# Two recurrent layers of attention and experts on one core: the turned rows and the output projection of a batch moved from the end of one step to the units 0 and 1 of the next

## The chip, the cores and the metric

The kernel runs on one core of a Trainium2 chip. The metric is the device time of one execution in microseconds, as the median of several runs. Lower is better.

## The reference, cut to what matters

Sixteen batches of 256 tokens with 128 channels pass through two layers. Each layer normalizes its input, computes an attention `s` and a mixture of experts `g`, and adds their product to the input.

```python
x = L0_attn_x                                  # (16, 256, 128)
xn = _layernorm(x)
s = _L0_attn_ref(xn, ...)                      # differential attention, 16 heads, causal
g = _silu(_L0_ffn_ref(xn, ...))                # top 2 of 8 experts
x = x + s * g
xn = _layernorm(x)
s = _L1_attn_ref(xn, ...)                      # window of 128, 16 heads of 8
g = _silu(_L1_ffn_ref(xn, ...))
x = x + s * g

# inside _L0_attn_ref, per batch and head
att = softmax(q1 @ k1.T) - lam * softmax(q2 @ k2.T)
y = att @ v
y = (y - mean(y)) / sqrt(var(y) + EPS) * (1 - LAMBDA_INIT)     # per head of 16 values
return y.reshape(B, T, 256) @ c_w
# inside _L1_attn_ref: out = softmax(windowed scores) @ v, then out @ wo.T + bo
```

## The kernel before

Each layer runs four parts one after the other: normalization, router, experts, attention. The experts leave their outputs in a list in HBM (`list_out`), from which the attention part later gathers the two rows of each token. The change touches only the attention part, `build_attention`, which is built once for each layer.

**Steps and units.** The attention part works on one batch of 256 tokens in each step. It is a software pipeline written out for every engine by itself: the function `schedule` calls the engine's `body` for the steps -3 to 16. The steps -3 to 0 are written out, the steps 1 to 12 are a loop (`Fori`) of three turns over four steps, and the steps 13 to 16 are written out again. A step has `UNITS` units, 12 in layer 0 (two attention maps `a`) and 6 in layer 1 (one map). In each unit TensorE computes two banks of scores for the row maxima of a batch ahead (`scores_for_max`, L986 and L987) and two banks of scores of the batch of this step (`scores`, the same lines). VectorE reduces the former to maxima (`search`, L1287) and ScalarE takes the exponentials of the latter (`exp`, L1188). In most units TensorE also multiplies probabilities and values (`weigh`, L1077 and L1080), which ScalarE copies out (`copy_weighed`, L1193).

**General uses.** All other products of TensorE share two PSUM banks, `G`. They are called general uses, and they take the two banks in turn, in the order of the table `ORDER`; the number beside each name is the unit at the end of which it stands. `general` lets TensorE start a use only when the use two before it has been copied out by ScalarE (`g_free`), and ScalarE copies them in the same order. The uses are: `qk0` and `qk1`, the projections to q and k of the batch three ahead (`project_qk`, L968; copied by `copy_qk`, L1169 and L1170 in layer 1); `v`, the values of the next batch (L975); `shift`, the turned negated maxima of the next batch (`turn_shift`, L1103; copied by L1216 and L1217); `turn{a}{qb}`, the weighed sums of map `a` turned so that queries lie on partitions (`turn_weighed`, L1088; copied by L1209); `rows`, the normalized rows turned back (`turn_rows`, L1096; copied by L1202 to `yT`); and `out`, the output projection (`project_out`, L1112 and in layer 1 L1115; copied by L1229 to `s_rows`).

**What follows a use.** `divide` on VectorE (L1336, in layer 1 L1345) stands in the unit that the table `DIVIDE` gives; it waits for the last turn of its map. In layer 0 GpSimd then computes the norm of each head (`head_norm`, L849 to L867), whose last instruction L867 writes `out_rows`; `turn_rows` waits for it. In layer 1 the division itself writes `out_rows`. `gate` on GpSimd (L898 and L900) multiplies `s_rows` by the experts' activated output and adds it to `x`; in layer 1 SyncE stores the result (`store`, L944). `fetch_ffn` (L877, four gathers by GpSimd's own DMA queue) and `mix_ffn` (L886, L889) bring the experts' output of a batch.

**The stack.** The copies of q and k are split on VectorE into three bf16 pieces (`split`, L1269, L1272, L1275, in the units of the table `SPLIT`). SyncE's queue then issues twelve transfers of them to the stack (`fill_stack`, L933), and ahead of these the two transfers of the split shifts (`split_shift` L1309, `fill_shift` L939), in this order in its queue. There is one buffer of pieces, so `copy_qk` of `qk0` waits until the fill of the batch before has landed (`stacked`).

In the order of GpSimd's queue a step was: mix of the last batch, head norm of the last batch (layer 0), fetch of this batch, gate of the last batch. The head norm of a batch, its turned rows and its projection were all in the same step: in layer 0 rows and projection stood in unit 11, the last, and in layer 1 in the units 4 and 5.

## Time and profile before

| | |
|---|---|
| median of 3 runs | 1562.79 us (1559.96 to 1567.36) |
| the profiled execution | 1560.15 us |
| its span, first to last instruction | 1558.4 us |
| TensorE busy | 1080.5 us, 69% |
| VectorE busy | 797.8 us, 51% |
| ScalarE busy | 756.5 us, 49% |
| GpSimd busy | 652.9 us, 42% |
| mean granted TensorE clock | 0.855 |

The shares are averages over parts with different limits. The attention part of layer 0 lies from about 335 to 896 us, that of layer 1 from about 1195 to 1558 us. PE is TensorE, DVE VectorE, ACT ScalarE, POOL GpSimd, SP SyncE, and SPq its DMA queue. In a row of the timeline the number in square brackets is the time for which the engine stood idle before the instruction, followed by what ended the wait.

### The profile page before, as it was taken

The page shows a single profiled execution, that of the slowest core. Times are in us where ns is not written, and L with a number is a line of the kernel's source. Part 1 is how long each engine was busy: PE and PEld are TensorE (multiplying, and loading weights), DVE is VectorE, ACT ScalarE, POOL GpSimd, SP SyncE. Part 2 cuts the span into 40 slices and gives each one's busy share as a digit, 9 for nine tenths or more (in the row PEclk, how much of TensorE's full clock was granted, in tenths as well). Part 3 has the DMA queues.
Part 4 walks back from the last instruction along what each step waited for, and adds up shares of the span by engine and source line. Part 5 has one row for each costly group of instructions (what it writes and reads, how often), then busy time and mean ns, then how long its engine had stood idle before and what let it go on. Part 6 is the DMA issues. An engine that isn't in the chain of part 4 may idle for free. (4 is left out here: it accounts for less than half of the span.)

```text
span 1558.4 us, 39725 instructions
## 1 busy us (share of the span) xinstructions
PE 1080.5 (69%) x12282; PEld 821.1 (53%) x12282; DVE 797.8 (51%) x1739; ACT 756.5 (49%) x1764; POOL 652.9 (42%) x868
## 2 busy tenths in 40 slices
PE   1400899858888788888888233009996678888886
PEld 1400899835655556555654122009996355555564
DVE  5411466447667666567562054115663555555561
ACT  2070456415667566676667022005553255555564
POOL 2277100010577677677767721760002013333344
PEclk9999999958899889898898555559998599999997
DMA  6061222132322232222400002312222222222220
GB/s 175 6 191 51 63 67 69 51 88 51 83 50 51 51 86 61 51 50 58 89 10 9 7 0 85 100 55 61 67 68 58 55 50 62 63 56 59 63 55 25
DMA packets 166094, 95.52 MB, mean 61 GB/s; under 512 B 18547, under 2 KB 159749, under 8 KB 165957
## 3 DMA queue, kind: packets, MB, share of 16 engines
q1 hardware_dynamic: 157764, 76.82, 19.0%
q0 software_dynamic: 8192, 16.79, 3.8%
q8 instruction: 96, 1.57, 0.4%
q14 instruction: 42, 0.34, 0.1%
HBM read 30.19 MB, written 24.64 MB: 35 GB/s over the span
## 5 line engine op out<-in xcount | busy, mean ns | idle before, releaser
L1287 DVE TENSOR_REDUCE at_maxima<-ps 128x2 f32<-128x512 f32 (+1 forms) x576 | 372.4, 685 | 224.2 <-PE ps L987 222.2
L1188 ACT ACTIVATE at_probs<-ps 128x512 f32<-128x512 f32 x576 | 322.4, 602 | 103.2 <-PE ps L987 98.3
L986 PE MATMUL ps<-tables 64*128 64x256 bf16 (+1 forms) x2304 | 232.6, 265 | 121.9 <-DVE at_maxima L1287 50.1
L615 ACT ACTIVATE ex_hid<-ps,ex_w 128x128 f32<-128x128 f32 x576 | 164.4, 368 | 251.0 <-PE ps L585 251.0
L987 PE MATMUL ps<-stack 64*128 64x128 bf16 (+3 forms) x3072 | 269.6, 262 | 0.0
L986 PEld LDWEIGHTS ps<-tables 64*128 64x128 bf16 x2304 | 96.1, 98 | 224.5 <-issue 189.8
L987 PEld LDWEIGHTS ps<-stack 64*128 64x128 bf16 (+1 forms) x3072 | 171.2, 102 | 9.1
L577 PE MATMUL ps<-ident,ex_rows 128*128 128x128 f32 x144 | 40.2, 279 | 195.2 <-DMA ex_rows<-list_in 195.1
L522 POOL DMA_INDIRECT list_in<-ex_rows,ex_slots x128 | 125.1, 977 | 100.9 <-DVE ex_slots L628 63.4
L646 DVE COPY ex_w<-ex_weights 128x1156 f32 x144 | 109.9, 763 | 106.4 <-issue 106.4
L585 PE MATMUL ps<-ex_rowsT,ex_w 128*128 128x128 f32 x1152 | 158.3, 282 | 0.1
L595 PE MATMUL ps<-ex_w,ex_hid 128*128 128x128 f32 x1152 | 153.6, 277 | 1.2 <-DVE ex_result L653 1.2
L877 POOL DMA_INDIRECT at_chosen_y<-list_out,at_slot x128 | 124.8, 975 | 55.6 <-issue 28.9
L585 PEld LDWEIGHTS ps<-ex_rowsT,ex_w 128*128 128x128 f32 x1152 | 143.1, 196 | 2.3 <-issue 0.7
L595 PEld LDWEIGHTS ps<-ex_w,ex_hid 128*128 128x128 f32 x1152 | 141.6, 194 | 1.5 <-issue 1.5
L1077 PE MATMUL ps<-at_probs,at_v 128*32 128x256 f32 x1536 | 130.9, 414 | 0.0
L577 PEld LDWEIGHTS ps<-ident,ex_rows 128*128 128x128 f32 x144 | 21.1, 146 | 197.0 <-issue 197.0
L898 POOL TENSOR_TENSOR at_s_rows<-at_s_rows,at_silu 128x256 f32<-128x256 f32 x32 | 23.5, 734 | 194.5 <-ACT at_s_rows L1229 194.1
L864 POOL TENSOR_TENSOR at_rstd<-at_stat,at_half 128x32 f32<-128x32 f32 x16 | 89.2, 5574 | 2.9 <-POOL at_stat L862 2.9
L1080 PE MATMUL ps<-at_probs,at_v 128*32 128x128 f32 x1536 | 80.7, 283 | 0.0
L626 DVE COPY ex_rows<-xn 128x128 f32 (+1 forms) x64 | 15.2, 237 | 123.8 <-DMA list_in<-ex_rows,ex_slots 123.2
L1269 DVE TENSOR_TENSOR at_whole<-at_whole,at_pieces 128x1024 f32<-128x1024 f32 (+1 forms) x32 | 31.1, 972 | 91.5 <-ACT at_pieces L1170 69.9
(166 smaller groups left out, 1555.6 us busy)
## 6 DMA issues: line engine op xcount, KB each, us to landing
stack<-at_pieces SPq DMA_DIRECT2D x192, 128.0 KB
stack<-at_pieces SPq DMA_DIRECT2D x192, 64.0 KB, 2.0
ex_rows<-list_in SPq DMA_DIRECT2D x144, 64.0 KB, 1.8
list_out<-ex_result SPq DMA_DIRECT2D x144, 64.0 KB, 1.5
list_in<-zero_tile SPq DMA_DIRECT2D x1, 4608.0 KB, 17.7
ex_weights<-in_L_w SPq DMA_DIRECT2D x4, 1024.0 KB, 7.4
ex_weights<-in_L_w SPq DMA_DIRECT2D x16, 256.0 KB, 7.1
x<-in_L_attn_x SPq DMA_DIRECT2D x4, 512.0 KB, 6.3
```

Of the source, the lines that this page charges most:

```text
L522: nc.gpsimd.indirect_dma_start(D["list_in"], bass.IndirectOffsetOnAxis(slots[q][k][:], 0), rows[q][:], None).then_inc(scattered[q], 16)
L585: last = nc.tensor.matmul(hid_ps[q % 2][:, hb * P:(hb + 1) * P], w[q][:, W1 + hb * P:W1 + (hb + 1) * P], rowsT[q % 2][:], start=True, stop ...
L595: last = nc.tensor.matmul(out_ps[q % 2][:, 0:C], hid[q % 2][:, hb, :], w[q][:, W2 + hb * C:W2 + (hb + 1) * C], start=(hb == 0), stop=(hb = ...
L615: last = nc.scalar.activation(hid[q % 2][:, hb, :], hid_ps[q % 2][:, hb * P:(hb + 1) * P], gelu, bias=w[q][:, B1 + hb:B1 + hb + 1])
L646: nc.vector.tensor_copy(w[q][:], weights[:, bass.ds(e, 1), :].rearrange("p o w -> p (o w)"))
L864: nc.gpsimd.tensor_tensor(rstd[:], stat[:], half[:], ALU.pow).then_inc(rstd_ready, 1)
L877: nc.gpsimd.indirect_dma_start(chosen_y[t][k][:], None, D["list_out"], bass.IndirectOffsetOnAxis(slot[:, i:i + 1], 0)).then_inc(gathered, 16)
L986: return nc.tensor.matmul(fine(bank, j), R.eye[tile, j, :], mask[tile], start=(j == 0), stop=True, skip_group_check=(j > 0))
L987: return nc.tensor.matmul(bank[:, j - 2, :], left(j - 2)[tile], right(j - 2)[tile], start=False, stop=True, skip_group_check=True)
L1077: nc.tensor.matmul(strip, v[p][:, 0, h, :], pr[:, part, at:at + SEQ], start=True, stop=False)
L1188: nc.scalar.activation(probs[:, (n // 3) % 2, n % 3, i * 512:(i + 1) * 512], t_bank[i], ACT.Exp, scale=SCALE).then_inc(t_free, 1)
L1287: nc.vector.tensor_reduce(by_half[:, h0:h0 + heads, a], s_bank[i].rearrange("p (m k) -> p m k", k=P * (late + 1)), AX.X, ALU.max).then_inc ...
```

## The change

In both layers `rows` and `out` of a batch move from the end of its step to the units 0 and 1 of the next step. The two turns of a map, which stood in one unit, now stand in two units that follow each other, and the divisions stand one or two units later (layer 0: map 1 from unit 3 to 4, map 0 from 9 to 11; layer 1: from 3 to 4). The gate of a batch moves one step later with them, to the head of GpSimd's step, and so does the store. The pipeline has one more step at its end. The steps that the loop covers go from 1 to 12, three turns, to 2 to 9, two turns; the rest is written out. No instruction on data is added or removed.

```diff
     if layer == 0:
-        ORDER = (("turn10", 2), ("turn11", 2), ("v", 4), ("qk0", 5), ("qk1", 6), ("shift", 8),
-                 ("turn00", 8), ("turn01", 8), ("rows", 11), ("out", 11))
-        DIVIDE = {3: 1, 9: 0}
+        ORDER = (("rows", 0), ("out", 1), ("turn10", 2), ("turn11", 3), ("v", 4), ("qk0", 5), ("qk1", 6),
+                 ("shift", 8), ("turn00", 9), ("turn01", 10))
+        DIVIDE = {4: 1, 11: 0}
...
     else:
-        ORDER = (("qk0", 0), ("qk1", 1), ("turn00", 2), ("turn01", 2), ("shift", 3), ("v", 4), ("rows", 4), ("out", 5))
-        DIVIDE = {3: 0}
+        ORDER = (("qk0", 0), ("rows", 0), ("qk1", 1), ("out", 1), ("turn00", 2), ("turn01", 3), ("shift", 3), ("v", 4))
+        DIVIDE = {4: 0}
...
-        if name in ("rows", "out", "last", f"turn{A - 1}0", f"turn{A - 1}1"):
+        if name in ("last", f"turn{A - 1}0", f"turn{A - 1}1"):
             return 0 <= step - 1 <= LAST
+        if name in ("rows", "out"):
+            return 0 <= step - 2 <= LAST
...
-    FIRST_FULL = 1
+    FIRST_FULL = 2
+    TURNS = (LAST - 2 - FIRST_FULL) // 4
...
-            with eng.Fori(0, (LAST - 3) // 4) as j:
+            with eng.Fori(0, TURNS) as j:
...
-            for step in range(LAST - 2, LAST + 2):
+            for step in range(FIRST_FULL + 4 * TURNS, LAST + 3):
...
                 if has(step, "out"):
+                    gate(step, step - 2)
+                if has(step, "last"):
                     mix_ffn(step - 1)
-                if has(step, "rows") and layer == 0:
-                    head_norm(step - 1)
+                    if layer == 0:
+                        head_norm(step - 1)
                 if has(step, "now"):
                     fetch_ffn(step)
-                if has(step, "out"):
-                    gate(step, step - 1)
...
                 if has(step, "out") and layer == 1:
-                    store(step - 1)
+                    store(step - 2)
...
-                    turn_rows(step, step - 1)
+                    turn_rows(step, step - 2)
...
-                    copy_out(step, step - 1)
+                    copy_out(step, step - 2)
...
-                    if has(step, "out") and n == SILU - 1:
+                    if has(step, "last") and n == SILU - 1:
                         tanh_ffn(step - 1)
...
-                    if has(step, "out") and n == SILU:
+                    if has(step, "last") and n == SILU:
                         twice_silu(step - 1)
```

## Rows read from the trace of the kernel before

**Rows 1.** Busy time (instructions), clock and DMA by stage: layer 0, layer 1.

```profile
398.00:895.00 497.00, 399.99 (x5628) 268.76 (x5616) 284.40 (x475) 310.27 (x622) 359.16 (x437) 0.85 0.21 49
1241.00:1558.00 317.00, 257.85 (x3184) 172.62 (x3183) 169.46 (x366) 179.71 (x428) 114.59 (x192) 0.93 0.21 53
```

**Rows 2.** Timeline of POOL in layer 0.

```profile
430.52 1.27 POOL L854 TENSOR_TENSOR at_y<-at_y 128x512 f32<-128x512 f32 x1 [2.82 <-DVE at_y L1336]
...
592.39 1.27 POOL L854 TENSOR_TENSOR at_y<-at_y 128x512 f32<-128x512 f32 x1 [0.95 <-DVE at_y L1336]
...
609.16 1.06 POOL L867 TENSOR_TENSOR at_out_rows<-at_y,at_rstd 128x512 f32<-128x512 f32 x1 [0.18 <-POOL at_rstd L864]
...
615.07 0.94 POOL L877 DMA_INDIRECT at_chosen_y<-list_out,at_slot  x1 [0.30 <-issue]
...
618.69 1.47 POOL L886 TENSOR_TENSOR at_chosen_y<-at_chosen_y,gate 128x128 f32<-128x128 f32 x4 [0.91 <-DMA at_chosen_y<-list_out,at_slot]
...
623.50 1.27 POOL L854 TENSOR_TENSOR at_y<-at_y 128x512 f32<-128x512 f32 x1 [2.28 <-DVE at_y L1336]
```

**Rows 3.** Timeline of PE in layer 0, from the rows to the turns.

```profile
610.28 1.12 PE L1096 MATMUL ps<-ident,at_out_rows 128*128 128x128 f32 x4 [0.62 <-POOL at_out_rows L867]
612.16 2.05 PE L1112 MATMUL ps<-wo,at_yT 128*128 128x128 f32 x8 [0.77 <-ACT at_yT L1202]
614.14 0.40 PE L986 MATMUL ps<-tables 64*128 64x128 bf16 x4
...
616.32 0.29 PE L986 MATMUL ps<-tables 64*128 64x128 bf16 x4
...
619.00 1.09 PE L1088 MATMUL ps<-ident,at_weighed_t 128*128 128x128 f32 x8
```

**Rows 4.** Timeline of one step of layer 1, engines in turn by time.

```profile
1383.96 0.47 ACT L1169 ACTIVATE at_whole<-ps,bqk 128x256 f32<-128x256 f32 x1 [4.55 <-DMA stack<-at_pieces]
...
1385.43 0.40 PE L986 MATMUL ps<-tables 64*128 64x256 bf16 x4 [2.92 <-ACT at_probs L1188]
...
1386.48 1.74 PE L1088 MATMUL ps<-ident,at_weighed_t 128*128 128x128 f32 x8
...
1387.63 1.28 DVE L1287 TENSOR_REDUCE at_maxima<-ps 128x2 f32<-128x512 f32 x2
...
1392.26 0.41 DVE L1309 TENSOR_TENSOR at_shift_p<-at_shift_t,at_shift_p 16x256 bf16<-16x256 f32 x1
...
1394.28 8.47 SPq L933 DMA_DIRECT2D stack<-at_pieces  x12
...
1402.69 0.70 PE L968 MATMUL ps<-xnT,wqk 128*128 x2
...
1404.37 0.47 ACT L1169 ACTIVATE at_whole<-ps,bqk 128x256 f32<-128x256 f32 x1 [4.08 <-DMA stack<-at_pieces]
```

**Rows 5.** Timeline of ACT in layer 1: the same copy in step 2 and step 12.

```profile
1281.58 0.47 ACT L1169 ACTIVATE at_whole<-ps,bqk 128x256 f32<-128x256 f32 x1 [3.39 <-DMA stack<-at_pieces]
...
1484.90 0.47 ACT L1169 ACTIVATE at_whole<-ps,bqk 128x256 f32<-128x256 f32 x1 [3.59 <-DMA stack<-at_pieces]
```

**Rows 6.** Timeline of PE and POOL at a jump back of the loop, layer 0.

```profile
648.95 0.40 PE L986 MATMUL ps<-tables 64*128 64x128 bf16 x4 [3.57 <-issue]
...
659.41 1.27 POOL L854 TENSOR_TENSOR at_y<-at_y 128x512 f32<-128x512 f32 x1 [5.83 <-DVE at_y L1336]
```

**Rows 7.** Timeline of DVE and POOL: one add beside a split, and without.

```profile
569.00 1.22 DVE L1269 TENSOR_TENSOR at_whole<-at_whole,at_pieces 128x1024 f32<-128x1024 f32 x1
...
569.13 1.39 POOL L849 TENSOR_TENSOR at_sq<-at_sq 128x128 f32<-128x128 f32 x1 [0.18 <-POOL at_sq L849]
...
793.39 0.45 POOL L849 TENSOR_TENSOR at_sq<-at_sq 128x128 f32<-128x128 f32 x1 [0.18 <-POOL at_sq L849]
```

**Rows 8.** Timeline of PE in layer 1: two pieces of the output projection.

```profile
1396.86 0.49 PE L1112 MATMUL ps<-wo,at_yT 128*128 128x128 f32 x2
...
1549.04 0.80 PE L1112 MATMUL ps<-wo,at_yT 128*128 128x128 f32 x2
```

## The prediction

> **What bounds the kernel now.** I read the busy time of the two attention stages first [rows 1]: about 497 us of layer 0 and 317 us of layer 1, and in neither is any engine full (TensorE 400 of 497 and 258 of 317, GpSimd 359 of 497). So each step is set by a loop of waits, not by an engine's sum, and the two layers have different loops.
>
> *Layer 0.* The start of a batch's head norm on GpSimd (L854) repeats every 31.1 us; from the step that starts it at 430.52 to the one at 623.50 there are six periods and 192.98 us, one of them with the jump back of the loop in it [rows 2]. The loop is: head norm, 592.39 to 610.22, 17.8 us; then TensorE, which already waits for it, turns the rows [rows 3]; then the projection, two units more, both turns of map 1, the search of unit 3, the division, and the next head norm at 623.50, 13.3 us after the last one's end. GpSimd by itself would allow less: its fetch issues end near 616.0, gate and mix end near 621.2, so it idles 2.28 us before 623.50 [rows 2]. So the cycle is 17.8 us of GpSimd plus 13.3 us of TensorE and its neighbours, and GpSimd's own floor is 2.3 us below it.
>
> *Layer 1.* The cycle is through SyncE [rows 4]. Put zero at 1383.96, where ScalarE's first copy of q (L1169) has waited 4.55 us for the stack's transfers, the twelve of the fill before. TensorE resumes at 1.47, the search of unit 2 begins at 3.67, the split of the shifts stands at 8.30, the twelve stack issues run from 10.32 for 8.47 us, and the next zero is at 20.41. TensorE is through with its work at 1403.39, one microsecond ahead of the next zero, and at this zero it waited 2.92 us in all: what stands there, ahead of the zero, is free. Over ten steps the period is 20.33 us [rows 5].
>
> **The change in layer 0.** Rows and output projection keep their place in the loop, except that unit 0 now stands ahead of the rows and unit 3 behind them: map 1's turns end at unit 3, the division follows at unit 4. So the number of units between the end of a head norm and the next is unchanged. What goes: the wait of 0.77 us between the rows and the projection [rows 3], since unit 1 stands between them, and the wait on one spot of two turns. What stays: 1.12 us rows, 2.05 us projection, three units, 1.09 us turns, the search and division. I lay it out from the end of the head norm, with the low clock behind the wait as in the row: rows to 1.2, unit 1 to 3.4 (2.2, like unit 0 in [rows 3], 614.14 to 616.32), projection to 5.4, unit 2 to 6.4, turn to 6.95, unit 3 with its weighing to 8.8, turn to 9.35, then 3.4 us to the head norm, as from 620.1 to 623.50: 12.8 instead of 13.3. Gain 0.5 us a step, 12 steps (2 to 13): **-6 us**. Bounds: nothing, if TensorE comes late to the rows, and 2.3 us a step, -28, where GpSimd's floor is reached.
>
> GpSimd's queue keeps its order around the circle (gate, mix, head norm, fetch); only the step's border moves between fetch and gate. The gate still waits for the projection's copy, now ready about 6 us after the head norm's end, when the fetch issues (5.8 us) have just gone out. The mix behind it waits for the gathers anyway. SyncE's order is the same too.
>
> The jump back costs 3.57 us of TensorE's time [rows 6] and makes that period 35.9 instead of 31.4 us (192.98 less 35.9, over five). The loop now runs twice instead of three times over four steps, so one of two jumps goes: **-4.5 us**. The other stands ahead of the wait for the head norm instead of behind it and is half hidden: **-2 us** (0 to -3.5). By the Trainium skill (Runtime: NRT & Kernel Launch, "Instruction fetch mechanics") a taken branch breaks the sequential prefetch and forces a fetch of its target; the trace agrees, and by that rule alone the sum would hold only these terms.
>
> A second effect is the place of VectorE's splits against the head norm. At 569.00 the split L1269 runs 1.22 us, and GpSimd's add beside it takes 1.39 us, where the same add takes 0.45 in a step without splits [rows 7]. The head norm starts one unit later against unit 7, so the split now meets another of its links, and the division of map 0, moved to unit 11, can meet the last link. I take zero: as many collisions as before, at other links; the ends are -1 and +0.7 us a step, that is -12 to +8. The Trainium skill (SBUF — State Buffer, "Who interferes with whom") has this as an exclusive lock: an operation with two SBUF inputs on VectorE and a reading one on GpSimd exclude each other, and the later one blocks. By it the moved division would add its 0.69 us wherever it starts first: about +8 us, the upper end.
>
> Layer 0 sums to **-12.5 us**.
>
> **The change in layer 1.** Here unit 0 and 1 stand at the zero itself, in the stretch where everything waits for the stack. The order of uses of the two general banks becomes q/k 0, rows, q/k 1, out. Q/k 1 now takes the bank of q/k 0, so TensorE can compute it only when ScalarE has copied q/k 0, after the zero; before, it was done at 1402.69, ahead of the zero [rows 4]. Behind it the projection, which needs the copy of the rows, and that stands in ScalarE's queue behind the copy of q/k 0. Queued behind both on TensorE are the scores of unit 2, and for these VectorE's search, the shift, the fill and the next zero.
>
> At what clock? TensorE's last work ahead of the wait ended at -0.98; take out the projection (four pieces at 0.42, 1.7) and q/k 1 (0.6) and it ends at -3.3. It resumes at 0.95: 4.2 us of waiting. After 2.92 us of waiting the row at 1386.48 shows eight transposes in 1.74 us where [rows 3] has 1.09: they ran at the level of 1.2 GHz. So I take the low clock for all of the burst: q/k 1 1.2 us, the projection 2.9 (0.80 for a pair against 0.49, [rows 8]), done at 5.05; half of unit 2's scores, and the search begins at 5.6 instead of 3.67. From there on the steps are as before (turn 1 at unit 3, ahead of the shifts, costs 0.55 us, but half of the earlier turns at unit 2 is gone). That is +1.9 us a step. Steps 2 to 12 have both the fill and the projection; the last delays only half: 10.5 times 1.9 is **+20 us**. Bounds: with the clock of 2.4 GHz throughout, q/k 1 and projection end at 3.35 and the search begins at 3.95, +0.3 a step, **+3**; with the low clock also over unit 2, unit 3 and their turns, +3 a step, **+31**.
>
> The jump back lies in layer 1 ahead of the zero, so most of its 3.57 us [rows 6] is hidden now; one goes, the other hides wholly: I give -1.5 for both (0 to -3.5). The store waits for a gate that is now early in the step. The last steps (no fill) hold the same work in another order: 0.
>
> **Sum.** -12.5 + 20 - 1.5 = +6. The profiled execution took 1560.15 us (span 1558.4); its sum is 1566. The median of the runs is 2.6 us above that execution, so I state 1562.8 + 6, rounded down: **1568 us**. A difference of 0.5%, 7.8 us, is about what a measurement of this kernel can tell.
>
> **The rivals.**
> *A, the clock stays up in layer 1 (chance 0.18).* For it: the granted clock is 0.93 over the stage [rows 1], so only a small part of a step ran low. Against: the wait becomes longer. Then +3 instead of +20: -11, **1552 us**. This ends faster.
> *B, layer 0 gives nothing but the jumps and loses to collisions (0.22).* For it: the units in the loop are the same in number, GpSimd's 17.8 us stay, and a division now lies at the head norm's end. 0 - 4.5 + 6 in layer 0, +18.5 in layer 1: +20, **1583**; half of that, +13, **1576**, if only the 0.5 us a step fail. It decides when the head norm grows by 0.5 us or TensorE arrives after it.
> *C, layer 0 falls to GpSimd's floor (0.1).* For it: 2.28 us of idle ahead of 623.50. Against: only 0.77 us of waiting is seen to go. -28 - 6.5 + 18.5 = -16, **1547**.
> *D, the change moves waits only (0.05)*: both loops keep their periods, only the jumps: -7, **1556**.
> My forecast, both mechanisms as laid out, has 0.45: its own range is 1559 to 1576.
>
> **Chances.** Faster by over 0.5% (under 1555): most of A, C and a little: 0.22. Slower by over 0.5% (over 1570.6): B and the upper third of my forecast: 0.38. Same: 0.40. The range that leaves two in ten out is 1551 to 1583.
>
> **What would show it.** Layer 0: head norms 30.6 us apart within the loop, 31.4 before; no wait of the projection for the copy of the rows; TensorE still waiting for L867 at the rows. One idle stretch of 3 us on TensorE for a jump in each layer, not two. Layer 1: zeros (L1169 behind the stack's DMA) 22.2 us apart instead of 20.3; q/k 1 after the zero; L1112 in pairs of 0.8 us; the search of unit 2 at 5.6. I am wrong if the pairs take 0.49 us there, if L1169 no longer waits for the DMA, or if the head norm's 17.8 us change.

## The result, and the profile after

The changed kernel takes 1576.12 us (median of 10 runs, 1567.34 to 1578.83), the kernel before, on the same chips, 1561.3. The ratio is 1.0082, 95% interval 1.0059 to 1.0104: slower by 0.8%. The profiled execution of after has a span of 1574.0 us, 15.6 more than before.

Where the 15.6 us lie is read from four marks: the last add to `x` in layer 0, the first zero of layer 1 (step -3), the zero of step 12, the end.

| stretch | before | after | difference |
|---|---|---|---|
| start to the last add to x in layer 0 | 894.89 | 874.41 | -20.5 |
| to the first zero of layer 1 | 303.03 | 302.99 | 0 |
| the zeros of steps -3 to 12 | 286.98 | 312.75 | +25.8 |
| zero of step 12 to the end | 73.5 | 83.9 | +10.4 |

One profile of each kernel stands in this table, and layer 0 differs between kernels whose layer 0 is the same: its last add stands at 890.9 and 891.5 us in e2 and e10, which have layer 0 as in before, and at 874.7 to 877.0 in e1, e3, e4, e7 and e11, which have it as in after. So some 17 us of the 20.5 are the change, the rest is chance.

(Lines of after are 3 higher than those of before in this part: L854 is now L857, L1169 is L1172.) The windows of the two attention stages, after; columns as in [rows 1]:

```profile
399.00:877.00 478.00, 382.26 (x5611) 253.03 (x5605) 293.88 (x474) 308.20 (x620) 372.48 (x437) 0.92 0.21 51
1221.00:1574.00 353.00, 280.16 (x3182) 188.76 (x3182) 181.94 (x365) 181.44 (x428) 120.41 (x192) 0.85 0.19 48
```

The granted clock has changed places: 0.85 to 0.92 in layer 0, 0.93 to 0.85 in layer 1.

**Layer 0.** POOL of after, one head norm and what follows, against [rows 2]:

```profile
591.21 1.48 POOL L852 TENSOR_TENSOR at_sq<-at_sq 128x256 f32<-128x256 f32 x1 [0.18 <-POOL at_sq L861]
...
595.40 6.50 POOL L867 TENSOR_TENSOR at_rstd<-at_stat,at_half 128x32 f32<-128x32 f32 x1 [0.18 <-POOL at_stat L865]
602.08 1.06 POOL L870 TENSOR_TENSOR at_out_rows<-at_y,at_rstd 128x512 f32<-128x512 f32 x1 [0.18 <-POOL at_rstd L867]
...
610.80 1.47 POOL L889 TENSOR_TENSOR at_chosen_y<-at_chosen_y,gate 128x128 f32<-128x128 f32 x4
...
614.07 1.27 POOL L857 TENSOR_TENSOR at_y<-at_y 128x512 f32<-128x512 f32 x1 [0.73 <-DVE at_y L1339]
```

The head norm that began at 584.38 ends at 603.14, and the next begins at 614.07. Before, that gap was 13.3 us; now it is 10.9, and GpSimd waits only 0.73 us in it: here it is at its floor. Two waits have shrunk, the one ahead of the head norm (2.28 to 0.73 us) and the mix's wait for the gathers (0.91 us at 618.69 in [rows 2], none at 610.80). The head norm itself grew from 17.8 to 18.76. VectorE beside its power operation L867:

```profile
595.36 1.20 DVE L1278 TENSOR_TENSOR at_pieces<-at_whole,at_pieces 128x1024 bf16<-128x1024 f32 x1
```

TensorE in the same stretch, against [rows 3]:

```profile
603.20 0.65 PE L1099 MATMUL ps<-ident,at_out_rows 128*128 128x128 f32 x4 [2.12 <-POOL at_out_rows L870]
...
605.34 1.16 PE L1115 MATMUL ps<-wo,at_yT 128*128 128x128 f32 x8
...
607.42 0.66 PE L1091 MATMUL ps<-ident,at_weighed_t 128*128 128x128 f32 x4
```

Rows in 0.65 us (1.12 before), projection in 1.16 (2.05 before), both at 2.4 GHz (the granted clock is 1.00 from 603 to 607) although TensorE waited 2.12 us just ahead; no wait for the copy of the rows is left. Not every step is like this one. Of the nine periods in steps 2 to 11 that hold no jump, six are 29.7 to 30.0 us, and three are 31.6 to 32.5, with GpSimd idle for 2.1 to 2.9 us ahead of the head norm. In these three TensorE did its rows, its projection or both at 1.2 GHz, as here:

```profile
694.31 1.12 PE L1099 MATMUL ps<-ident,at_out_rows 128*128 128x128 f32 x4 [2.12 <-POOL at_out_rows L870]
...
698.19 2.08 PE L1115 MATMUL ps<-wo,at_yT 128*128 128x128 f32 x8
...
707.92 1.27 POOL L857 TENSOR_TENSOR at_y<-at_y 128x512 f32<-128x512 f32 x1 [2.86 <-DVE at_y L1339]
```

The mean of the nine is 30.5 us, against 31.4 before. The jump back, PE and POOL:

```profile
540.73 0.40 PE L989 MATMUL ps<-tables 64*128 64x128 bf16 x4 [4.31 <-issue]
...
554.42 1.27 POOL L857 TENSOR_TENSOR at_y<-at_y 128x512 f32<-128x512 f32 x1 [2.21 <-DVE at_y L1339]
```

The period with it is 33.8 us, 3.3 over that mean and 4.0 over the short ones (4.5 over the mean in before): one jump is gone, and most of the other is still paid.

**Layer 1.** The zeros of steps 2 and 12, against [rows 5]:

```profile
1262.51 0.47 ACT L1172 ACTIVATE at_whole<-ps,bqk 128x256 f32<-128x256 f32 x1 [4.94 <-DMA stack<-at_pieces]
...
1490.15 0.47 ACT L1172 ACTIVATE at_whole<-ps,bqk 128x256 f32<-128x256 f32 x1 [3.86 <-DMA stack<-at_pieces]
```

227.64 us for ten steps: 22.76 each against 20.33. But there are two kinds of step. The windows of two that follow each other, from zero to zero:

```profile
1401.10:1422.58 21.48, 16.44 (x224) 11.11 (x216) 13.30 (x26) 11.52 (x28) 8.27 (x13) 1.00 0.22 57
1422.58:1446.08 23.50, 19.61 (x208) 13.54 (x208) 12.82 (x25) 11.92 (x29) 8.28 (x13) 0.78 0.21 52
```

Where the granted clock stays at 1.00 the step takes 21.5 us, where it is 0.78 on the mean 23.5. (One step fits neither: step 6, behind the jump back, took 23.3 us at 0.97. TensorE was still catching up there, and its projection began 3.2 us after the zero instead of 1.5.) PE and DVE in the second, against [rows 4]:

```profile
1423.56 0.67 PE L971 MATMUL ps<-xnT,wqk 128*128 x2 [2.73 <-ACT at_pieces L1173]
1424.07 0.39 PE L1115 MATMUL ps<-wo,at_yT 128*128 128x128 f32 x2
...
1425.12 0.80 PE L1115 MATMUL ps<-wo,at_yT 128*128 128x128 f32 x2
...
1426.57 0.61 PE L989 MATMUL ps<-tables 64*128 64x256 bf16 x4
...
1427.63 0.69 DVE L1290 TENSOR_REDUCE at_maxima<-ps 128x2 f32<-128x512 f32 x1 [1.03 <-PE ps L990]
...
1428.39 1.11 PE L1091 MATMUL ps<-ident,at_weighed_t 128*128 128x128 f32 x4
...
1432.01 0.66 PE L1091 MATMUL ps<-ident,at_weighed_t 128*128 128x128 f32 x4
...
1433.60 0.41 DVE L1312 TENSOR_TENSOR at_shift_p<-at_shift_t,at_shift_p 16x256 bf16<-16x256 f32 x1 [0.68 <-ACT at_shift_p L1220]
```

After the wait of 2.73 us q/k 1 and the first pair run at 2.4 GHz (0.39), then everything at 1.2 GHz until about 1431.6: the rest of the burst, unit 2, its turn (1.11), unit 3. The search begins 5.05 us after the zero, the split of the shifts 11.02 (8.3 before). In a step with the clock up it stands at 9.35.

The two kinds differ in whether TensorE waits at the zero. In the six low steps (2, 3, 5, 7, 9 and 10) it waited 2.3 to 3.2 us for ScalarE's copy of q/k 0, and the clock fell 1.4 to 2.2 us after the zero. In the steps 4, 6, 8 and 11 it came late to the zero, waited less than 0.6 us, and ran at 2.4 GHz up to the shifts (in step 6 from 1.6 us after the zero on). It came late because the clock had been at 1.2 GHz in the last units of the step before, and in step 6 because of the jump back too. So a low stretch at the end of one step spares the next one its own, unless it is short, as at the end of step 9. The same steps of e7 and e11 (below) fall apart in the same way: where TensorE waited 0.8 us or more for the copy of q/k 0, the split of the shifts stands at 12.6 to 14.3 us in e7 and 10.6 to 12.9 in e11, and where it waited less than 0.6, at 11.0 to 11.7 and 9.0 to 9.2. This is read from thirty steps and was not forced by an experiment.

**The last steps.** ScalarE's row of exponentials for the keys outside (`zero_exp`, L1227) of the last batches:

```profile
1504.00 0.22 ACT L1227 ACTIVATE at_zero_exp<-at_shift 128x16 f32<-128x16 f32 x1 [2.85 <-DVE at_out_rows L1348]
...
1521.75 0.22 ACT L1227 ACTIVATE at_zero_exp<-at_shift 128x16 f32<-128x16 f32 x1 [2.94 <-DVE at_out_rows L1348]
```

It waits for the division of the batch before, which is now one unit later; before, the same waits were 2.07 and 1.66 us. TensorE is also slower here: from the zero of step 12 to the last add it is busy for 64.98 us at a granted clock of 0.86 (714 instructions), before for 58.20 us at 0.91 (704).

### The profile page after: what moved, and what is told of

It is laid out like the page before. It is cut to its first block and busy times, and to the rows that moved or that the text cites. A ratio compares the mean times of both kernels' runs of the same rounds, so it can differ in the third digit from the quotient of the medians.

```text
span 1574.0 us, 38698 instructions
## 1 busy us (share of the span) xinstructions
PE 1088.1 (69%) x12282; PEld 822.6 (52%) x12282; DVE 820.2 (52%) x1739; ACT 757.4 (48%) x1764; POOL 671.6 (43%) x868
## 3 DMA queue, kind: packets, MB, share of 16 engines
q1 hardware_dynamic: 157764, 76.82, 18.5%
## 5 line engine op out<-in xcount | busy, mean ns | idle before, releaser
L989 PE MATMUL ps<-tables 64*128 64x256 bf16 (+1 forms) x2304 | 236.3, 268 | 117.0 <-DVE at_maxima L1290 49.7
L990 PE MATMUL ps<-stack 62*128 62x256 bf16 (+3 forms) x3072 | 269.5, 262 | 0.0
L990 PEld LDWEIGHTS ps<-stack 62*128 62x128 bf16 (+1 forms) x3072 | 172.9, 103 | 12.0
L577 PEld LDWEIGHTS ps<-ident,ex_rows 128*128 128x128 f32 x144 | 21.1, 146 | 197.0 <-issue 197.0
L901 POOL TENSOR_TENSOR at_s_rows<-at_s_rows,at_silu 128x256 f32<-128x256 f32 x32 | 23.5, 734 | 229.4 <-ACT at_s_rows L1232 229.1
L867 POOL TENSOR_TENSOR at_rstd<-at_stat,at_half 128x32 f32<-128x32 f32 x16 | 96.3, 6020 | 2.9 <-POOL at_stat L865 2.9
L971 PE MATMUL ps<-xnT,wqk 128*128 128x256 f32 (+1 forms) x192 | 65.8, 462 | 29.2 <-ACT at_pieces L1173 19.8
## 6 DMA issues: line engine op xcount, KB each, us to landing
list_in<-zero_tile SPq DMA_DIRECT2D x1, 4608.0 KB, 17.7
```

Source lines behind the costliest of these rows:

```text
L867: nc.gpsimd.tensor_tensor(rstd[:], stat[:], half[:], ALU.pow).then_inc(rstd_ready, 1)
L989: return nc.tensor.matmul(fine(bank, j), R.eye[tile, j, :], mask[tile], start=(j == 0), stop=True, skip_group_check=(j > 0))
L990: return nc.tensor.matmul(bank[:, j - 2, :], left(j - 2)[tile], right(j - 2)[tile], start=False, stop=True, skip_group_check=True)
```

## The experiments

All ratios are to the kernel before on the same chip (1560.2 to 1561.8 us). "Late zero" is short for a step whose next zero comes 2.2 us or more after the last stack issue of SyncE ended; 1.6 is usual. Twelve steps (0 to 11) are counted in each kernel.

**e1, the change in layer 0 alone; e2, in layer 1 alone.** A variable `LAG` per layer takes the place of the fixed 2, with the tables of before in the other layer:

```diff
+    LAG = 2 if layer == 0 else 1        # e2: layer == 1
...
-            return 0 <= step - 2 <= LAST
+            return 0 <= step - LAG <= LAST
...
-    FIRST_FULL = 2
+    FIRST_FULL = LAG
```

> The change in layer 0 alone; layer 1 as before. Theory (two changes of opposite sign): the profile after the change has layer 0's part about 20 us shorter, so this kernel takes about 1541 us, ratio 0.987 to the kernel before. Rival (the two layers act on each other through the loop or the code's length, or the layer 0 gain is a quirk of one execution): between 1550 and 1561 us.

> The change in layer 1 alone; layer 0 as before. Theory: about +36 us, 1597 us, ratio 1.023: some 26 us up to step 12 (2.4 us a step) and 10 us in the steps 13 to 17. Rival (my recorded sum): +18.5 us, 1580 us.

Measured: e1 1550.58 us, ratio 0.9932 (0.9912 to 0.9952); e2 1591.08, ratio 1.0203 (1.0176 to 1.023). Layer 0 is a gain, layer 1 the loss, and the two add up to within 3 us (18 us against 15). e1 missed its forecast of 1541 and lies at the edge of its rival's range, that of a code that acts on the other layer by its length. Layer 0 of e1 again ends 19.5 us early (875.35). But e1 is only 11 us faster: layer 1, whose instructions are those of before, took 298.3 us between the zeros of steps -3 and 12 instead of 287.0. Its splits of the shifts stand at 8.1 us in most steps, as before; what differs is nine late zeros against one, which hold 9.8 of the 11.3 us. The DMA view of e1, from 1 us ahead of the end of the last stack issue (1367.06) to the next zero, has this in its part on queues and issues:

```profile
q1 hardware_dynamic: 747, 0.34, 34.3%
q8 instruction: 1, 0.02, 2.5%
...
stack<-at_pieces SPq DMA_DIRECT2D x2, 64.0 KB, 2.9
```

The same stretch in a step of before (1401.76 to 1404.37), whose zero came in time:

```profile
q1 hardware_dynamic: 671, 0.31, 45.3%
...
stack<-at_pieces SPq DMA_DIRECT2D x2, 64.0 KB, 2.0
```

One packet of instructions (16 KB, 0.9 to 1.6 us on one of the 16 DMA engines) is there where the stack's last transfers take 2.9 us to land, and absent where they take 2.0. Of the 20 late zeros of before, e1, e5 and e6, 16 have such a packet that starts between 0.4 us ahead of the issue's end and 0.6 us behind it; of the 28 in time none has, and the one packet in this stretch starts 1.1 us after the issue's end. The other four late zeros (steps 4 and 8 of e1 and e5) are of another kind. They stand at the jumps back, the last transfer has landed after 1.45 us as usual, and ScalarE waits for TensorE's q/k 0, which the jump holds up:

```profile
1328.10 0.47 ACT L1175 ACTIVATE at_whole<-ps,bqk 128x256 f32<-128x256 f32 x1 [2.47 <-PE ps L974]
```

In before the zeros at the two jumps are in time (1.62 and 1.75 us).

**e3, zero_exp in four buffers, waiting for the division of two batches back; e4, both turns in unit 2 and the division in unit 3 again.**

```diff
# e3
-            zero_exp = [sb(f"zero_exp{p}", [P, HEADS]) for p in range(2)]
+            zero_exp = [sb(f"zero_exp{p}", [P, HEADS]) for p in range(4)]
...
-                    lone_wait(act, divided, b - 1)
+                    lone_wait(act, divided, b - 2)
# e4
-        ORDER = (("qk0", 0), ("rows", 0), ("qk1", 1), ("out", 1), ("turn00", 2), ("turn01", 3), ("shift", 3), ("v", 4))
-        DIVIDE = {4: 0}
+        ORDER = (("qk0", 0), ("rows", 0), ("qk1", 1), ("out", 1), ("turn00", 2), ("turn01", 2), ("shift", 3), ("v", 4))
+        DIVIDE = {3: 0}
```

> The whole change, but zero_exp in layer 1 has four buffers, so that ScalarE's copy of the shifts at unit 3 waits for the division of the batch before last and no longer for the one that the change moved to unit 4. Theory (the steps after the last fill lose their 10 us because ScalarE stands behind this division for 2.9 us in each of five steps): 7 to 10 us of the 15 come back, 1566 to 1569 us. Rival (the last steps lose by the longer fall of the clock or by the order of the projection): less than 3 us come back.

> The whole change, but in layer 1 both turns stand in unit 2 and the division in unit 3 again; rows and projection stay in the units 0 and 1. Theory (the moved division makes the last steps' loss, the burst behind the stack's wait makes the rest): the last steps get back 7 to 10 us, the steps 2 to 12 lose up to 0.5 us each by four more transposes at the low clock: 1566 to 1574 us. Rival (the loss hangs on rows and projection alone): 1576 us or more.

Measured: e3 1582.08 (ratio 1.0134, 1.0108 to 1.016), e4 1580.51 (1.0105, 1.0067 to 1.0144). In e3 the stretch from step 12's zero to the last add is 74.3 us against 77.6 in after and 67.3 in before: the wait stood on the path, but it is only a third of that loss. Up to step 12 e3 took 322.6 us instead of 312.75, with the split of the shifts at about 12 us in six of the ten steps from 2 to 11. In all ten TensorE waited at the zero (2.1 to 4.3 us), so that none had the clock up throughout. e4 gains nothing in the end (79.4) and takes 318.3 ahead of it; it puts four more transposes in unit 2 besides, so it does not show the division by itself. Both missed their forecasts (1566 to 1569 and 1566 to 1574): the late division explains 3.3 us at the end and not the loss.

**e7, the products of layer 1's projection done twice.**

```diff
-                for qb in range(QB):
+                for qb in (0, 1, 0, 1) if layer else (0, 1):
```

> The kernel after, with the products of layer 1's output projection done twice (the second set writes the same bank again with the same values), so four more pairs of 0.4 to 0.8 us in each step, all in unit 1, behind the zero. My theory: whatever stands between the zero and the scores of unit 2 is on the cycle of layer 1, so the added products cost their whole time: at the pair's 0.80 us of the lower clock 1.6 us a step, and where the added work lets the clock rise earlier, a part comes back; the period of the steps 2 to 12 goes from 22.8 to 23.9 to 24.4 us, and the total from 1576 to 1588 to 1598 us. Rival: the cycle is not on TensorE there (it is on ScalarE's copies, or on the landing of the transfers), and the added work is hidden: 1576 to 1580 us. Second rival: the low clock, not the work, is what costs; with more work ahead of unit 2 the clock is back at 2.4 GHz before it, the search of unit 2 comes no later, and the time falls to 1566 to 1574 us.

Measured: 1606.52, ratio 1.0292 (1.026 to 1.0324). ACT and PE of e7 (zeros of steps 2 and 12, one burst):

```profile
1262.33 0.47 ACT L1172 ACTIVATE at_whole<-ps,bqk 128x256 f32<-128x256 f32 x1 [3.62 <-DMA stack<-at_pieces]
1507.82 0.47 ACT L1172 ACTIVATE at_whole<-ps,bqk 128x256 f32<-128x256 f32 x1 [4.30 <-DMA stack<-at_pieces]
```

```profile
1385.75 0.46 PE L1115 MATMUL ps<-wo,at_yT 128*128 128x128 f32 x2
...
1387.42 0.80 PE L1115 MATMUL ps<-wo,at_yT 128*128 128x128 f32 x2
...
1390.32 0.61 PE L989 MATMUL ps<-tables 64*128 64x256 bf16 x4
```

The period is 24.55 us, 1.8 more than after and just over the 23.9 to 24.4 forecast: the burst stands on the cycle. Here the added set stands from 1387.42 to 1390.32, 2.9 us. It did not lift the clock: unit 2 is still at 0.61. The total went above the range, because the last steps pay too (90.7 against 77.6 us), which I had not counted.

**e11, q/k 1 ahead of the rows again, so that it doesn't need q/k 0's bank.**

```diff
-        ORDER = (("qk0", 0), ("rows", 0), ("qk1", 1), ("out", 1), ("turn00", 2), ("turn01", 3), ("shift", 3), ("v", 4))
+        ORDER = (("qk0", 0), ("qk1", 1), ("rows", 1), ("out", 2), ("turn00", 2), ("turn01", 3), ("shift", 3), ("v", 4))
```

> The kernel after, with layer 1's order of uses q/k 0, q/k 1, rows, out (rows at unit 1, out at unit 2, both turns at units 2 and 3 behind it). So q/k 1 takes the other bank and can be computed ahead of the zero again, as in before; the projection, four pieces of work behind the copy of the rows, moves one unit on. My forecast's theory, that of the 2.4 us a step that layer 1 lost the burst q/k 1 plus projection at 1.2 GHz ahead of unit 2's scores is the cause: with q/k 1 out of it 0.7 to 1.2 us a step come back, and the projection still costs its 1.0 to 1.6 us ahead of the shifts: period 21.5 to 22.1 us against 22.8, total 1563 to 1570. Rival: the low clock of the first units is the cause, whatever stands in them, since TensorE waits 3 us at the zero in either order; then 22.5 to 23 us and 1573 to 1578. Second rival: the rows' wait for their bank moves behind ScalarE's copy of q/k 1 and is later than before: 1580.

Measured: 1576.77, ratio 1.0104 (1.0061 to 1.0147), the period of steps 2 to 12 22.74 us: nothing gained. The forecast (1563 to 1570) failed, and the rival of the low clock, 22.5 to 23 us and 1573 to 1578, is what came. PE of e11 in a step whose split of the shifts stands at 9.2 us, then in the next, where it stands at 12.85:

```profile
1354.85 0.46 PE L1115 MATMUL ps<-wo,at_yT 128*128 128x128 f32 x2
...
1358.85 0.66 PE L1091 MATMUL ps<-ident,at_weighed_t 128*128 128x128 f32 x4
```

```profile
1372.96 0.41 PE L1099 MATMUL ps<-ident,at_out_rows 128*128 128x128 f32 x2 [1.65 <-ACT at_pieces L1173]
...
1375.42 0.77 PE L1115 MATMUL ps<-wo,at_yT 128*128 128x128 f32 x2 [0.78 <-ACT at_yT L1205]
...
1382.59 1.12 PE L1091 MATMUL ps<-ident,at_weighed_t 128*128 128x128 f32 x4
```

The same instructions, 3.6 us apart at the split of the shifts. Counted from the zero the projection starts at 3.64 us in the first and at 3.44 in the second, so the difference arises behind it, where the clock differs: 0.46 and 0.66 against 0.77 and 1.12. Ahead of it the second step waited twice (1.65 and 0.78 us), the first, behind the jump back, did not. So not which use stands in the burst, but how much of TensorE's work between the zero and the shifts falls into the low stretch sets the step.

**e5, the change in layer 0 alone and its three splits two units later; e6, that with layer 1's zero_exp in four buffers and a loop of two turns in layer 1; e12, e6 with layer 0's loop written out.**

```diff
# e5, layer 0
-        SPLIT = {7: (0,), 8: (1,), 9: (2,)}
+        SPLIT = {9: (0,), 10: (1,), 11: (2,)}
# e6, layer 1 with the order of before
-    FIRST_FULL = LAG
+    FIRST_FULL = 2
...
-            zero_exp = [sb(f"zero_exp{p}", [P, HEADS]) for p in range(2)]
+            zero_exp = [sb(f"zero_exp{p}", [P, HEADS]) for p in range(4)]
...
-                    lone_wait(act, divided, b - 1)
+                    lone_wait(act, divided, b - 2)
# e12: no Fori in layer 0
```

> The change in layer 0 alone, as in e1_layer0_only, and there the three splits of q and k (L1269, L1272, L1275 of before) two units later, in units 9, 10 and 11 instead of 7, 8 and 9. My theory: layer 0 now runs at GpSimd's floor (period 29.8 us, GpSimd's idle time ahead of the head norm 0.7 us), and of the head norm's 18.8 us one microsecond is paid to the splits that meet its first adds and the start of its power operation. With the splits elsewhere the head norm takes 17.8 to 18.2 us, the period is 29.0 us, and over 12 steps 7 to 10 us go: 1541 to 1545 us, against 1550.6 in e1. Rival: the later fill of the stack, now starting at unit 11 instead of unit 9, holds up the scores of the next batch or the copy of its q and k, and the period stays at 29.8 or grows to 31: 1550 to 1565 us. Second rival: the splits only meet other links of the head norm, whose time stays at 18.8: 1550 us.

> As e5_layer0_split, and in layer 1, whose order of uses is that of before, zero_exp has four buffers and its copy waits for the division of two batches back instead of one; the loop of both layers starts at step 2, so it has two turns instead of three. My theory: in the last four steps of layer 1 ScalarE's wait for the division (1.7 to 2.1 us a step in before, 2.9 to 3.0 in the kernel after) stands on the path, and without it those steps are 1 us shorter each; one jump less gives 0 to 2. So 3 to 6 us under e5. Rival: the wait stands where ScalarE has time to spare, since the steps up to 12 are bound by the stack and the last by TensorE, and only the jump shows: 0 to 2 us under e5. Second rival: as in e3_four_zero, the earlier exponentials shift TensorE's clock or the fill, and layer 1 up to step 12 is 5 us longer: e5 plus 1 to 3.

> e6_layer0_split_zero with layer 0's loop written out; layer 1's loop stays. My theory: the one jump back that is left in layer 0 (the period with it is 31.9 us against 30.4) goes: 1.5 to 4 us under e6. But the program ahead of layer 1 is now longer, so the blocks of code fall elsewhere against layer 1's steps; where they fall on the end of the stack's issues, up to 8 us come back. So 1534 to 1536 us, or up to 1544, and the count of zeros that come 2.3 us or more behind the last issue must tell which (2 of 12 in e6). Rival: written-out code costs as much as the jump: 1537 to 1539 at the same count.

Measured: e5 1547.2 (0.9901, 0.987 to 0.9933), e6 1537.62 (0.9846, 0.9816 to 0.9876), e12 1534.92 (0.9846, 0.9806 to 0.9887). e6 and e12 beat both kernels.

In e5 the head norm fell further than expected (16.4 to 17.8 us, here 17.55), but layer 0 ended where it did in e1 (874.58 against 875.35). POOL and SP of e5:

```profile
591.23 1.41 POOL L853 TENSOR_TENSOR at_stat<-at_sq 128x32 f32<-128x32 f32 x1 [0.20 <-POOL at_sq L853]
...
609.97 1.47 POOL L890 TENSOR_TENSOR at_chosen_y<-at_chosen_y,gate 128x128 f32<-128x128 f32 x4 [2.47 <-DMA at_chosen_y<-list_out,at_slot]
```

```profile
598.30 9.48 SPq L939 DMA_DIRECT2D stack<-at_pieces  x12
```

The later fill now spans all four gathers (issued 600.90 to 605.73), and the mix waits for them, 2.47 us here and 0.5 to 3.0 in the other steps, where in after it waited for nothing in eleven of twelve steps. The microsecond won in the head norm is lost there: the rival's sign, at another place than it named. The total of 1547.2 missed the forecast of 1541 to 1545.

In e6 layer 1 fell by two things. The stretch behind step 12's zero is 63.5 us to the last add against 67.6 in e5: 4.1, the four steps of 1 us of the theory. And 244.4 us between the zeros of steps 0 and 12 against 253.8: one late zero instead of nine, most likely because the two turns had moved the code, which I had not foreseen. e12 ends layer 0 3.2 us earlier (871.56), inside what was expected for the jump; layer 1 stayed at 244.7 us although it has five zeros between 2.26 and 3.13: its fills were shorter (17.7 us from the zero where the packet comes at their end, 18.3 to 18.7 in e6). Counting late zeros alone doesn't give the time.

**e8, before with its loops at two turns.**

```diff
-            with eng.Fori(0, (LAST - 3) // 4) as j:
+            with eng.Fori(0, 2) as j:
...
-            for step in range(LAST - 2, LAST + 2):
+            for step in range(9, LAST + 2):
```

> The kernel before, with its loop of two turns over four steps instead of three, steps 9 to 16 written out; nothing else differs. It prices a jump back by itself. My forecast's price: 4.5 us in layer 0 and 0 to 1.5 in layer 1, so 1556 to 1557 us against 1561.5, ratio 0.996 to 0.997. Rival: the jump is paid only as TensorE's idle time, which the next wait for GpSimd takes back; then 1561 us, ratio 1.000. Second rival: the longer program makes the fetch of instructions cost elsewhere, and nothing or a loss of 1 to 3 us is seen.

Measured: 1553.61, ratio 0.9966 (0.994 to 0.9992), as forecast. The parts hide more: layer 0 ends at 885.29, 9.6 us early (though e10 and e2, with layer 0 as in before, ended at 891.54 and 890.94, so 3 to 4 us of that are chance), and layer 1 has seven late zeros instead of one and takes 5 us more between steps -3 and 12.

**e9, e5 with 176 empty instructions on TensorE's queue ahead of layer 1's attention; e10, before with 80.**

```diff
+            if layer == 1:
+                for _ in range(176):        # e10: 80
+                    pe.sem_inc(passed, 1)
             schedule(pe, body)
```

> e5_layer0_split with 176 instructions that do nothing but count (sem_inc on a semaphore that nobody waits for) on TensorE's queue ahead of layer 1's attention; no work and no wait differs. Ground: in before, e1, e5, e6 and e8 together the next zero comes 2.3 to 3.6 us after the end of the last stack issue in 28 of 60 steps, and in each of these a packet of queue q8 (instruction, 16 KB, 0.9 to 1.5 us on one of the 16 DMA engines) starts within 0.6 us of that end; where none does, it comes 1.5 to 1.9 us after it. My theory: this packet, a block of TensorE's own code, stands ahead of the last stack transfer on its DMA engine; where in a step it falls is set by how many instructions were issued before, modulo the block. The 176 instructions shift the blocks against the steps to the places they have in before, where 1 of 12 zeros is late: late zeros from 9 of 12 to 1 or 2, layer 1 from step 0 to step 12 8 to 11 us shorter, the whole 1537 to 1541 us against 1547. Rival: the late landings come from the store of x or the gathers, and the packet is only a bystander: still 9 late of 12, 1547 to 1550 us.

> The kernel before with 80 such instructions on TensorE's queue ahead of layer 1's attention; nothing else differs. My theory: the blocks of code now fall where they fall in e5, at the end of the stack's issues: late zeros from 1 of 12 to 7 to 9 of 12, layer 1 8 to 11 us longer, the whole 1568 to 1573 us against 1561, though not one instruction with work was added. Rival: it is not the blocks of code: 1561 to 1563 us, one late zero.

Measured: e9 1568.24 (1.0061, 1.0036 to 1.0086), e10 1578.58 (1.0113, 1.0071 to 1.0154). Windows from the zero of step 0 to that of step 12: before, e10, e5, e9.

```profile
1241.53:1484.90 243.37, 199.19 (x2478) 133.86 (x2478) 139.71 (x296) 137.99 (x330) 81.96 (x139) 0.94 0.23 58
```

```profile
1249.61:1504.24 254.63, 208.11 (x2480) 138.03 (x2480) 140.16 (x296) 139.32 (x331) 83.27 (x139) 0.91 0.22 56
```

```profile
1220.73:1474.51 253.78, 205.99 (x2478) 137.15 (x2478) 139.33 (x296) 138.92 (x330) 82.31 (x139) 0.91 0.22 56
```

```profile
1248.75:1491.85 243.10, 199.37 (x2478) 134.11 (x2478) 139.35 (x295) 138.85 (x330) 82.76 (x139) 0.94 0.23 58
```

In this stretch the kernels swapped: before 243.4 to 254.6 us with one late zero becoming eight, e5 253.8 to 243.1 with nine becoming one. The work is the same. That is the theory's 8 to 11 us in both directions. But it is not all the landing of the transfers: two of the eight and two of the nine are zeros at a jump back (2.96 to 3.93 us), and they hold 3.6 of the 8.5 us by which the zeros of e10 came later, and 3.2 of the 9.7 by which those of e9 came earlier. So the place of the code sets what a jump costs too. Both totals missed all the same (1537 to 1541 and 1568 to 1573 were expected), because the empty instructions were not free. PE ahead of layer 1, in e5 and in e9:

```profile
1175.85 2.07 PE L974 MATMUL ps<-xnT,wqk 128*128 128x256 f32 x4 [4.62 <-POOL at_v L913]
```

```profile
1203.85 2.04 PE L974 MATMUL ps<-xnT,wqk 128*128 128x256 f32 x4 [31.77 <-issue]
```

27.15 us for 176 of them; in e10 the wait was 17.05 instead of 4.61, 12.4 for 80. Taking 27 off, e9 would stand at 1541; taking 12 off, e10 at 1566 (both estimates from these rows).

The same count over all fourteen kernels, 168 steps: in 42 a packet of q8 starts between 0.4 us ahead of the last stack issue's end and 0.8 us behind it, and in every one of these the next zero comes 2.2 to 3.7 us after that end. The ten other late zeros all stand at a jump back and wait for TensorE's q/k 0. In no other step is the zero late. The expectation of e9 took the two kinds for one; the packet within 0.6 us that it sees in each late zero is there only in the first kind.

## Why the prediction was right, and where not

The forecast of 1568 had the mechanisms of both layers and the sign between them, and the result lies 8 us above it inside the range, on the slow side. Its terms:

- **Layer 0, 0.5 us a step, -6.** Too small. I kept the low clock behind the wait "as in the row". With unit 0 ahead of the rows it stayed at 2.4 GHz in most steps: 0.5 us less in the rows, 0.9 less in the projection. Six of nine gaps fell to 10.9 to 12.1 us instead of 12.8, the others stand at 12.3 to 13.7. The mean period fell by 0.9 us, and that with a longer head norm. The sign that I named, 30.6 us against 31.4, came nearly as stated (30.5), but it is a fall of 0.8 us, and the sum counted only 0.5. In the short steps GpSimd's idle time is down to 0.7 to 1.5 us, which is rival C's sign (the row of 2.28 us of idle, [rows 2]), to which I gave 0.1; its price of -28 did not come.
- **The gathers, no term.** "The mix behind it waits for the gathers anyway" was wrong. In before the mix waited 0.9 to 2.3 us for them in each step, after in one of twelve (0.3 us). In before the gathers were issued (611.2 to 615.1) within the fill of the stack (607.2 to 615.2), after they began (604.1) as it ended (605.4). e5, whose fill spans them again, has the wait back.
- **Collisions, 0.** All but one of the head norms of the steps 0 to 11 grew by 0.9 to 1.4 us, past the upper bound of 0.7 a step. The links that met a split were an add (1.48 instead of 0.72 us) and the power operation (6.50 instead of 5.47). The Trainium skill (SBUF — State Buffer, "Who interferes with whom") calls this a lock in which the later operation blocks. The trace agrees for the power operation, which started 0.04 us behind the split at 595.36 and took 1.03 us longer. e5's small add (1.41 us beside a split of 1.20, some 0.24 without) was held up too, although its record starts 0.1 us ahead of the split's.
- **The jumps.** One gone, -4.5: borne out by e8 at least (layer 0 ends 5.7 to 9.6 us earlier). The other was to be half hidden, -2: only 0.5 to 1.2 us of it were, its period is 3.3 to 4.0 us longer; e12 got 3.2 back by taking it out.
- Layer 0 together: -20.5 against -12.5, some 17 as the mean over kernels with the same layer 0.
- **Layer 1, 1.9 us a step, +20.** The chain was right: q/k 1 and the projection behind the zero, in front of unit 2 (e7 shows them on the cycle). The burst was cheaper than I took (3.0 us, partly at 2.4 GHz, the search at 5.05 instead of 5.6; TensorE's wait ahead of it 2.3 to 3.2 us instead of 4.2), but in the low steps the clock then stayed low through unit 2 and most of unit 3, which I had only as the upper bound. Mixed over both kinds of step it is 2.4 us, +24.3 from step 2 to 12 (7 of these ten steps took 23.0 us or more, 3 took 20.8 to 21.5).
- **The last steps, 0.** This term failed: +10.4. "The same work in another order" overlooked that these steps are on TensorE's path, and that ScalarE's zero_exp waits for the division now one unit later. e3 gave back 3.3 of it. TensorE's longer busy time at the lower clock (64.98 us against 58.20, 6.8 more) is of the size of the rest, and e7 shows that the projection's work stands on the path there; no run separates the two.
- **Jumps in layer 1, -1.5.** Nothing was saved that can be seen. In before the steps with the two jumps took 21.1 and 21.0 us, about 1 us over the mean of the others. The one left in after makes its zero late (2.42 us, ScalarE waits for TensorE's q/k 0), and the step behind it took 23.3 us with the clock up, where 20.8 to 21.5 are usual.

Of the rivals, A (the clock stays up in layer 1) holds in 3 of the 10 steps. B, layer 0 gives nothing, is wrong: the result lies at its time of 1576 for another reason. So the time was met by two errors of opposite sign: 8 us too little gain in layer 0, 18 us too little loss in layer 1 and at its end (36.2 against 18.5). That the sum came within 8 us of the result is in part luck. One of the prediction's own signs of being wrong, a change of the head norm's 17.8 us, did come: the collisions stood at zero in the sum.

One cause of differences had no term at all: where TensorE's blocks of code land. The changed kernel has three late zeros (steps 1 and 10 by a packet, step 5 by the jump back), before one. By e9 and e10 the place of the code alone is worth up to 11 us in layer 1, nearly as much as the result. It does not carry the result here: the loss is in steps without late zeros as well (23.3 us with the next zero at 1.6).

What stays open: whether TensorE's wait at the zero is what drops the clock, since no run takes the wait away alone; and which DMA engine a block of code takes, so that the order of packet and transfer on it is argued from the coincidence and from e9 and e10, not seen.

## What to carry to other kernels

Treat the two loops of a kernel apart. Here the stage whose loop runs through a compute engine gained from work put between TensorE's waits, and the one whose loop runs through a transfer lost by work put directly behind it, since that work and the next units ran at the lower clock in most steps. Before a change of less than 1% is believed or dismissed, look at whether the code blocks (queue q8) moved against the tightest transfer. Here the change in layer 0 alone gave 0.7%; with its splits later, four buffers of zero_exp and a shorter loop it came to 1.5% under before.

## What the runs showed of the hardware

- A 16 KB block of TensorE's code passes through the same DMA engines as data. Where it started between 0.4 us ahead of the last stack issue's end and 0.8 us behind it (42 of 168 steps), the next zero came at 2.2 to 3.7 us instead of 1.6. The Trainium skill (Runtime: NRT & Kernel Launch, "Instruction fetch mechanics") has the crossing of a 16 KiB boundary as mostly hidden. For TensorE that may be so; for a transfer that others wait for it was not. With 80 empty instructions ahead of the layer, twelve steps went from 243.4 to 254.6 us, by five more such landings and by two jumps back that now held up the zero.
- An instruction that only raises a semaphore took TensorE's queue 0.155 us (27.15 over 176, 12.4 over 80).
- A jump back of the attention loops left TensorE idle for 2.2 to 5.6 us. The period around it in layer 0 was longer than the mean of the others by 4.5 us in before, 3.3 in after and 1.4 in e6.
- The same step with the same instructions had the clock at 2.4 GHz where TensorE had waited less than 0.6 us at the zero, and fell to 1.2 GHz where it had waited 2.3 to 3.2 us (after, steps 2 to 11).
- Where the fill of twelve transfers spanned the gathers, GpSimd waited 0.9 to 2.3 us (before) and 0.5 to 3.0 us (e5) for them; where it ended as they began (after), for nothing in eleven of twelve steps.
